# An attention block with experts on one core: value products computed ahead of the weighing, with the turned probabilities as the stationary operand

## What is computed

```python
h1 = adaln(x, t, norm1)                  # x is layer-normed first
x  = mha(h1, h1, wq, wk, wv, wo, bo) + x # 16 heads of 64
h2 = adaln(x, t, norm2)
x  = mha(h2, context, ...) + x
h3 = adaln(x, t, norm3)
x  = glu_ff(h3, w1, b1, w2, b2) + x      # gelu gate, 512 wide
# then a layer norm, a router that picks 2 of 8 experts per token, and the expert FFNs
```

## Time and profile before

| what | us |
|---|---|
| median of 3 runs (2133.06 to 2137.06) | 2136.75 |
| span of the profiled execution | 2124.9 |
| TensorE busy in the span | 2039.6 (96%) |
| ScalarE, VectorE, GpSimd busy | 1386.2, 1323.4, 1071.9 |

### The profile page before, as it was taken

How to read it: one execution, slowest core, us unless ns; L and a number is a source line. 1 busy time by engine, 2 the same in 40 slices (tenths; PEclk the granted TensorE clock), 3 DMA queues, 4 the chain that set the end, 5 groups by cost and what they waited for, 6 DMA issues and landing times. The chain is left out here.

```text
span 2124.9 us, 38735 instructions
## 1 busy us (share of the span) xinstructions
PE 2039.6 (96%) x11068; PEld 1337.7 (63%) x11068; DVE 1323.4 (62%) x3389; ACT 1386.2 (65%) x2659; POOL 1071.9 (50%) x1198
## 2 busy tenths in 40 slices
PE   7899999999999999999999999999999889899996
PEld 5455555555555555555555565555555558799996
DVE  5554657676767676767676666666656545455565
ACT  4566666676667676767676767676766666566663
POOL 2444444636363637363737373737363445556664
PEclk9999999999999999999999999999999999999998
DMA  4110111121111111111111111111122312222256
GB/s 153 45 26 25 50 35 51 46 50 45 49 45 50 46 53 45 49 45 49 45 49 45 49 45 51 47 48 52 44 54 64 96 48 57 58 56 72 60 185 215
DMA packets 136321, 127.35 MB, mean 60 GB/s; under 512 B 14665, under 2 KB 110569, under 8 KB 136234
## 3 DMA queue, kind: packets, MB, share of 16 engines
q1 hardware_dynamic: 127466, 109.11, 18.7%
q0 software_dynamic: 8768, 17.20, 2.5%
HBM read 86.63 MB, written 40.67 MB: 60 GB/s over the span
## 5 line engine op out<-in xcount | busy, mean ns | idle before, releaser
L1928 POOL TENSOR_TENSOR pr<-pr,sm 128x512 f32<-128x512 f32 x256 | 277.7, 1098 | 483.7 <-DVE sm L1462 483.7
L1126 ACT ACTIVATE kp<-ps 128x512 f32<-128x512 f32 x512 | 298.9, 601 | 179.5 <-PE ps L283 176.2
L834 PE MATMUL ps<-tt,V 128*128 128x512 f32 x768 | 380.3, 593 | 3.5 <-ACT tt L1126 3.5
L1452 DVE TENSOR_REDUCE mx<-ps 128x8 f32<-128x512 f32 x256 | 176.8, 691 | 306.3 <-PE ps L783 306.3
L1126 ACT ACTIVATE tt<-ps 128x512 f32<-128x512 f32 x512 | 275.2, 591 | 40.2 <-PE ps L813 39.6
L783 PE MATMUL ps<-kp,hf 128*64 128x256 f32 x2048 | 276.8, 392 | 6.9 <-DVE pr L1455 3.9
L283 PE MATMUL ps<-cT,M 128*128 128x512 f32 x768 | 262.0, 464 | 0.0
L783 PEld LDWEIGHTS ps<-kp,hf 128*64 128x64 f32 x2048 | 124.4, 136 | 196.9 <-DVE pr L1455 142.4
L1126 ACT ACTIVATE pt<-ps 128x512 f32<-128x512 f32 x256 | 153.6, 600 | 141.4 <-PE ps L795 139.1
L283 PE MATMUL ps<-hk,M 128*128 128x512 f32 x768 | 242.2, 438 | 0.0
L941 PE MATMUL ps<-xT,wt 128*128 128x128 f32 (+1 forms) x1728 | 221.9, 278 | 4.0 <-DVE wt L1753 4.0
(11 more groups left out here) (235 smaller groups left out, 3470.3 us busy)
## 6 DMA issues: line engine op xcount, KB each, us to landing
mod<-emb_s SPq DMA_DIRECT2D x96, 256.0 KB, 4.3
xr<-rows_s SPq DMA_DIRECT2D x144, 66.0 KB
cb<-y_s SPq DMA_DIRECT2D x32, 256.0 KB
x_in<-in_x_dram SPq DMA_DIRECT2D x16, 256.0 KB, 4.4
xn_s<-x_in SPq DMA_DIRECT2D x16, 256.0 KB, 2.1
res<-xn_s SPq DMA_DIRECT2D x16, 256.0 KB, 2.8
c_in<-in_ctx_dram SPq DMA_DIRECT2D x16, 256.0 KB, 4.7
y_s<-res SPq DMA_DIRECT2D x16, 256.0 KB, 2.0
```

Source lines behind the costliest of these rows:

```text
L834: mm = nc.tensor.matmul(psO[:], Vw[a][:, g * HG + head_at(h), :], tt[:, h, :], start=(g == 0 and h == 0), stop=ends)
L1126: return nc.scalar.activation(o, i, ACT.Copy)
L1452: nc.vector.tensor_reduce(mx[:, p % 2, :], heads(psS[p % 2][:]), AX_X, ALU.max).then_inc(max_done, 1)
L1928: tensor(v, v, sm[:, p, :].unsqueeze(2).broadcast_to([P, HG, 64]), ALU.mult).then_inc(prob_done, 1)
```

## The change

The values are now computed before they are weighed. In slot (i, u), behind the weighings, stand eight `values` products for this unit: for each sequence s the tokens (`hf0`, or `cf` for the context, 128 x 64) are stationary and 512 columns of `Vw` move, twice, into the two 64-partition halves of a bank. ScalarE copies them to `vp`. `weigh` then takes the turned probabilities as the stationary operand, 64 columns at a time, and 128 columns of `vp` as the moving one, and accumulates over heads straight into `psO` in token rows. So `project`, the fp32r splits on GpSimd, ScalarE and VectorE, the `oT` copies of the attentions, `back1` and `back2` are gone; the attention bias is added by GpSimd (`add_bias`) to the residual that has been loaded. `scores` moves 8 heads x 64 keys at once. On TensorE a slot is now: four turns in a block, scores and weighings alternating, values, keys with the stages. Turns use three banks, the fourth turn the first of them again; values and keys share a ring of 6, 6, 4 or 3 banks (`RINGS`), and a product waits until the one before it in its bank has been copied. The GLU output has a bank of its own (`psF`).

The core of the diff:

```diff
+            def values(i, u, s, bank):
+                a, g = divmod(u, 2)
+                src = hf0 if a == 0 else cf
+                for e in range(2):
+                    heads = slice(HG * g + HH * e, HG * g + HH * e + HH)
+                    mm = nc.tensor.matmul(bank[64 * e:64 * e + 64, :], src[:, 64 * s:64 * s + 64],
+                                          Vw[a][:, heads, :].rearrange("p h d -> p (h d)"), start=True, stop=True)
+                mm.then_inc(v_done, 1)
             def scores(i, u, p):
                 for s in range(2):
-                    for j in range(2):
-                        mm = nc.tensor.matmul(psS[p % 2][64 * j:64 * j + 64, :]...[:, :, s, :],
-                                              hf[u // 2][:, cols], kp[:, j * HH:(j + 1) * HH, cols], start=True, stop=True)
+                    mm = nc.tensor.matmul(psS[p % 2][64 * s:64 * s + 64, :].rearrange("p (h k) -> p h k", h=HG),
+                                          hf[u // 2][:, cols], kp[:, :, cols], start=True, stop=True)
             def turn(i, u, p):
-                    pe.wait_ge(pt_done, n)
+                for w in left_in(i, u, psT[p]) if p < 3 else [(pt_done, n - 2)]:
+                    wait(w)
                 pe.wait_ge(prob_done, n + 1)
             def weigh(i, u, p):
-                for s in range(2):
-                    nc.tensor.matmul(pst[s][:], tm[rows, p, :], pt[rows, p % 2, :], start=True, stop=True).then_inc(t_done, 1)
-            def project(i, u, h):
+                pe.wait_ge(vp_done, v_count(i, u, 2 * p + 1))
+                for m in range(4):
+                    for s in range(2):
+                        mm = nc.tensor.matmul(psO[64 * s:64 * s + 64, p * D:(p + 1) * D], pt[:, p, m * P + 64 * s:m * P + 64 * s + 64],
+                                              vp[:, 2 * p + s, m * D:(m + 1) * D], ...)
             def slot(i, u):
+                if last:
+                    for p in range(NT):
+                        turn(li, lu, p)
+                    scores(i, u, 0)
                 for p in range(NT):
+                    if here and p < NT - 1:
+                        scores(i, u, p + 1)
                     if last:
+                        weigh(li, lu, p)
+                    for s in range(2 * NT):
+                        product("v", s)
                 for h in range(HG):
-                        next_key(h)
+                        product("k", h)
-                        project(li, lu, h - 2)
# ScalarE
             def slot(i, u):
+                if last:
+                    for p in range(NT):
                         turn_hi(li, lu, p)
                 if here:
+                    for p in range(NT):
+                        exp(i, u, p)
+                    for s in range(2 * NT):
+                        values_hi(i, u, s)
             def context(c):
+                copy(cf[:], psM[:]).then_inc(cx_f, 1)
                 copy(cT[:, 0, :], psM[:]).then_inc(cx_hi, 1)
# GpSimd
+            def add_bias(c, a):
+                pool.wait_ge(ld_y1 if a else ld_xn, 16 * c + 16)
+                tensor(row[:], row[:], b_o[:, a, :]..., ALU.add).then_inc(bias_done[a], 1)
```

More of the change, by code:

```diff
@@ L165, in pixart_block_moe @@
                 res = sw("res", [P, NT, D])
+                y1r = sw("y1r", [P, NT, D])
+                y2r = sw("y2r", [P, NT, D])
                 gl = sw("gl", [P, 2, CT], F32R)
@@ L756, in wait, with keys @@
                 pe.wait_ge(*w)
-            def keys(i, u, h):
+            def keys(i, u, h, bank):
                 a, g = divmod(u, 2)
@@ L1003, in slot @@
-                    if p == 0 and u == 0 and ok(i - 3) and not c_last(i - 3):
-                        glu_down(i - 3, FT - 1)
-                def next_key(h):
-                    if h < len(RINGS[u]):
-                        bank = RINGS[u][h]
-                        if last:
-                            for w in [(pt_done, 4 * seq(li, lu) + 4)] if bank is psT else [] if bank in psS else t_free(li, lu, 3 if bank is psH else 2):
-                                wait(w)
-                        if here and bank in psS:
-                            pe.wait_ge(sub_done, 4 * seq(i, u) + 4)
-                    keys(*after(i, u), h)
@@ L1015, in slot, with product @@
-                if last:
-                    weigh(li, lu, 3)
+                        weigh(li, lu, p)
+                def product(kind, x):
+                    made, banks = products(i, u), RINGS[u]
+                    j = made.index((kind, x))
+                    bank = banks[j % len(banks)]
+                    if j >= len(banks):
+                        wait(emptied(i, u, *made[j - len(banks)]))
+                    elif bank in psT and last:
+                        pe.wait_ge(pt_done, 4 * seq(li, lu) + (4, 2, 3)[psT.index(bank)])
+                    elif bank in psS and here:
+                        pe.wait_ge(sub_done, 4 * seq(i, u) + 3 + psS.index(bank))
+                    elif bank in psS and isinstance(i, int) and i == NC:
+                        pe.wait_ge(eu_act, 3 * E)
+                    elif bank is psF and u < 2 and ok(i - 3):
+                        pe.wait_ge(f2_out, i - 2)
+                    if kind == "v":
+                        values(i, u, x, bank)
+                    else:
+                        keys(*after(i, u), x, bank)
@@ L1969, in add_x @@
                 pool.wait_ge(ld_xa, 16 * c + 16)
-                tensor(tmp[:], tmp[:], res[:], ALU.add).then_inc(u_done, 1)
+                tensor(y2r[:], y2r[:], res[:], ALU.add).then_inc(u_done, 1)
+            def add_bias(c, a):
+                if first(c):
+                    pool.wait_ge(ld_b, 64)
+                pool.wait_ge(ld_y1 if a else ld_xn, 16 * c + 16)
+                row = y2r if a else y1r
+                tensor(row[:], row[:], b_o[:, a, :].unsqueeze(1).broadcast_to([P, NT, D]), ALU.add).then_inc(bias_done[a], 1)
             def pairs(ap, axis):
```

429 lines of the change are left out of this document (129 added, 300 removed).

## The result

The changed kernel takes 2152.98 us (median of 4 runs, 2152.64 to 2159.47) against 2135.30 us of the kernel before in the same comparison: ratio 1.0093, 95% interval 1.0074 to 1.0112. A second comparison of the same two kernels gave 2151.15 against 2130.88, ratio 1.0099 (1.0075 to 1.0123). It is slower by 0.9 to 1.0%, some 18 to 20 us. The forecast was 2147 us: slower, but by 10 us against the 2136.75 that it started from.

A forecast was written before the change was run, and what follows sets the result against it. TensorE's work was taken as the bound: 6.1 us saved against 7.1 us of waits a round gave +7 us on 2124.9. With 11.9 from span to median and a 0.25 us a round margin: 2147 us, range 2095 to 2200.

The forecast's parts named there:

- the front: First part of a slot on TensorE: transposes, scores, weighings, eight values and shape changes; forecast 15.85 us.
- the walk: Stepping through the engines' in-order chains beside TensorE's keys and scores to find new waits: 7.1 us a round.
- loads that don't hide: Weighings: 32 pairs a slot of 0.061 us weight loads stay exposed, +125 us, 2272 us; chance 0.07.
- no pairing: Weighings: no two products run side by side, +225 us, 2372 us; chance 0.03.
- issue rate of 0.98 us: Weighings: an issue limit of 0.98 us a tile, +26 us, 2173 us; counted inside the main forecast's range.
- glu_up(0), slot 2: TensorE waits for ScalarE's and VectorE's ln3 copy and split with only the fourth key to do: 1.1 us a round.
- turns of slot 3: Slot 2 into 3: the fourth turn waits for the first bank's `pt` copy behind ScalarE's chain: 2.9 us a round.
- glu_down and glu_up(3), slot 3: ScalarE's three table loads of 1.28 us delay these steps on TensorE: 1.6 us a round.
- backf and turns, slot 0: backf waits for the context's bank beside two keys, 0.75 us, and turns 0.1: 0.85 us a round.
- fourth scores, slot 1: norm4, 1.03 us between VectorE's first and second subtraction, delays the fourth scores: 0.6 us a round.
- The early slots: Slots of the first rounds, with few of the waiting chains: about -6 us in total.
- The price of a wait: Each us of wait a round costs 13 us in total; below about 6.3 us of waits the kernel gains.

The follow-up runs named there:

- the combined kernel: Changed kernel with all wait-removing edits except halved values, plus first-norm copies moved: ratio 0.9769; with the first norm also ahead of the router steps, 0.964.
- the last kernel: All those wait-removing edits on the changed kernel, plus VectorE's first norm ahead of the router steps: 2037.2 us against 2114.1 of the kernel before, ratio 0.964.
- the second group: Runs on one chip: changed kernel again, fourth bank, earlier transposes, all edits together; the kernel before took 2130.9 us.
- the first group: Runs on one chip: changed kernel with earlier gate exponential, earlier first gelu, later fourth norm or halved values; the kernel before took 2112.4 us.

## Why the prediction was right, point by point

**The sign and the cause.** It forecast that TensorE's work falls by 6.1 us a round, that waits of 7.1 take its place, and named each. The trace has all of them, and the combined kernel shows that without them the changed kernel is 3.6% ahead. The net per round was forecast as +1.0 (1.25 with the margin) and is +1.6. The signs that were named came: the front takes 15.9 us, glu_up(0) starts 1.75 us behind the ln3 transpose's end (1.7 forecast), the fourth turn 4.25 us behind the last key of slot 2 (4 forecast), glu_up(3) 1.0 late. TensorE's busy share in the rounds is 95.1% by the rows and 93% by the starts (99.0 of 106.4); 93 was forecast.

**The number was luck in part.** The forecast was +10 us, measured are +17.7 and +20.3. The span was forecast at 2135 (2124.9 + 7 for the walk + 3 for the margin) and is 2150.9, 16 us more. The forecast then added 11.9 us from the span to the median, as in the kernel before, where the changed kernel needs 2.1; so 2147 came within 6 us of 2153. The sign, too, hung on 1 us in 7: the kernel with one step of ScalarE moved stands at 0.9978.

**The front.** 15.85 us forecast. In slot 2 it takes 1.91 us for the turns with the change of shape behind them (1078.35 to 1080.26; 1.76 + 0.15 forecast) and 13.95 us from there to the first key (1080.26 to 1094.21), 15.86 together. The weighing, for which no row of the trace before existed, was taken at 0.88 and is 0.86 to 0.88. The values with the way out of the shape take 6.97 for 6.98, scores and weighings 6.98 for 6.96. The two dear rivals, loads that don't hide (+125 us) and no pairing (+225), are out, and so is the issue rate of 0.98 us.

The first of these was the rule against the change: had 32 loads a slot of 0.061 us stood in the open, scores would follow scores at 1.74 + 0.49 = 2.23 us; the trace has 1.74. The Trainium skill, "TensorE: Matmul & The Clock Gate", Part 3, says under what overlaps that a load overlaps a running product only if the row group differs; these loads fill all rows, so the trace disagrees with that sentence. (The same part elsewhere also allows a load into the background weight buffer; which of the two happens here no run shows.)

**Work saved: 6.1 us forecast, 5.8 shown.** The round of 106.4 less waits of 7.4 is 99.0 us of work, against 104.8 before.

**Waits** of one round, in us. "Trace" is from the starts: the distance less what the same group takes where nothing is late (0.70 a key, 0.87 a weighing, 0.44 a turn).

| wait | forecast | trace | round shorter when removed |
|---|---|---|---|
| glu_up(0), slot 2 | 1.1 | 1.05 | 1.4 with backf, and a new wait |
| turns of slot 3 | 2.9 | 2.9 (about 0.9 to 1.0 each of three) | 1.7 (two of them), 0.4 to 0.5 (the fourth turn's) |
| glu_down and glu_up(3), slot 3 | 1.6 | 0.13 + 0.26 + 1.0 + 0.28 | 1.6 |
| backf and turns, slot 0 | 0.85 | 0.76 + 0.45 | with glu_up(0) |
| fourth scores, slot 1 | 0.6 | 0.57 | 0.7 |
| sum | 7.1 | 7.4 | 6.4 in the last kernel |

The walk found every place, and the sizes to 0.4 us. In one place the wait it named is not the one that stands there: it put 2.9 us on the fourth turn behind the first tile's copy, and the trace splits the sum over the first, second and fourth turn, since the same chain of ScalarE stops TensorE already at the banks of the sixth and seventh key (their copies start at 1103.40 and 1104.86, the turns at 1104.04 and 1105.49). The one term that was too small is the turns of slot 0, 0.45 for 0.1. Less work saved by 0.3 and more waits by 0.3 make the +1.6 a round where +1.0 was forecast; the margin of 0.25 was set for that and too small by half.

**The early slots: wrong by 6.6 us.** The forecast gave them -6. At the first turn the kernel was already 7.6 us behind (61.9 against 54.3), at the start of the 13 rounds 0.6. I overlooked that the value work of a unit moves ahead by a slot: the first unit's eight values stand before the first turn, and the last unit leaves no projections behind it. Slots (2, 2) and (2, 3) were forecast at +2 and are +2.0 (57.3 us against 55.3); they lie inside the window of the 13 rounds. Behind the window -2 was forecast. From its end to the first expert tile, before and changed:

```profile
1589.30:1744.20 154.90, 138.17 (x647) 80.61 (x645) 90.96 (x235) 98.02 (x169) 63.70 (x63) 0.98 0.27 76
```

```profile
1610.40:1761.80 151.40, 128.28 (x856) 79.44 (x856) 82.63 (x220) 93.67 (x159) 50.49 (x53) 0.99 0.25 70
```

TensorE has 9.9 us less work there and the stretch is 3.5 us shorter. The second execution of the changed kernel doesn't repeat that: it takes 156.7 us, with TensorE busy for 136.0 at a granted clock of 0.91. So the clock can take back more than this stretch gains.

**The account of the spans**, 2150.9 - 2124.9 = 26.0: up to the rounds +0.6, 13 rounds +20.5, up to the expert tiles -3.5, expert tiles +8.3, end +0.1. The medians differ by 17.7 and 20.3. The 8.3 us of the expert tiles are of the size by which this phase differs between kernels with the same code there on one chip (357 to 366 us in the second group), and the profile of the kernel before lies 11.9 us under its median where that of the changed kernel lies 2.1 under its own, so I don't count them as the change's. Why this phase takes 340 to 346 us in two of the groups and 357 to 367 in the other runs stays open; the rows show less busy time of TensorE where it is short, and mostly a higher granted clock.

**The price of a wait** ("13 us for each us a round"). The totals against the kernel before go along with the rounds, from rounds of 105.9 (1.0062 and 1.0065) over 105.7 (1.0025), 104.6 to 105.0 (0.9955 to 0.9993) and 101.8 (0.9769) to 100.0 (0.964). But 13 us for each us would give 1.0052 for rounds of 105.7, 0.9985 to 1.0 for the three kernels of the first group with 104.6 to 104.9, 0.981 and 0.970 for the last two: they are 0.2 to 0.6% faster than that. The traces show where: up to the first expert tile they take 141.0 to 150.2 us behind the 13 rounds, the kernel before 155.0 and 156.1. The forecast counted -2 for that stretch; how much of it is the edits' and how much the chip's is open. The turning point was put at 6.3 us of waits a round; by the measured work it is 5.8, and the four kernels with 1.4 to 1.8 us of the 7.4 taken away, just at that point, stand within 0.5% of the kernel before.

## What to carry to other kernels

When an engine that is 99.9% busy is given less work, count what that work covered: here 5.8 us of saved work a round uncovered 7.4 us of waits in the in-order chains of ScalarE and VectorE, and each was in the old timeline, as the distance from a product to its copy, split and next product. The way to the gain is then not another product but the order of the small steps on the engines that are busy for only 63 and 68% of the rounds: a table load put into idle time, a norm ahead of a router step that waits. Make all of them before judging such a change; one alone gives back 0.4 to 1.8 us a round, and the last wait (the first norm's transposes) came up only behind the others, in the kernels whose transposes had moved.

## What the runs showed of the hardware that I had not expected

- A table load on ScalarE doesn't wait for the product that its activation reads: in the kernel with the early gelu it starts at 981.11, right behind the copy, and the gelu waits another 0.55 us for TensorE. So a load can be hidden by setting its activation ahead of an idle gap. For an earlier wait of the same step it does wait (the load at 1129.62, 0.34 us idle for VectorE's `gl`).
- The idle time in the rows understates a wait of TensorE by some 0.2 us (from the changed kernel to the last one 4.7 us of idle time went, and the round fell by 6.4), and a short one doesn't show at all: 0.13 us by the starts had nothing in the rows.
- 16 passes of 128 columns with 16 loads of 64 columns, paired over the two halves of the output, take 0.86 to 0.88 us, as long as one full fp32 product of 0.86.
- The same last phase takes 340 to 346 us in two groups of runs and 357 to 367 in the others, at a granted clock of 0.98 to 0.99 and 0.96 to 0.98, while the middle rounds of one kernel agree to 0.1 us at clock 1.00.
